# A bias subtraction in two parts, a low part ahead of statistics, a weight split behind a wait, and an activation copy moved by one place

## The reference

```
x = layernorm0( attn0(x, ctx) @ Wo + bo + x ) * gamma + beta     # 32 heads of 16, 8 key/value heads, mask
for i in (1, 2):                                                  # 16 heads of 128
    h = layernorm(x) * scale_i + offset_i
    q, k, v = h @ wq + bq, ctx @ wk + bk, ctx @ wv + bv
    k, v = concat(k, bias_k), concat(v, bias_v)                   # one extra key and value
    x = x + softmax(q @ k.T / sqrt(128)) @ v @ wo + bo
x = x + gelu(layernorm(x) @ w_fc1 + b_fc1) @ w_fc2 + b_fc2        # 512 -> 2048 -> 512
```

## Time and profile before

| | |
|---|---|
| time, median of 3 runs | 2440.11 us (2439.7 to 2440.71) |
| profiled execution, whole | 2439.39 us |
| its span, first to last instruction | 2437.6 us |
| TensorE busy | 2363.2 us, 97% of the span |
| TensorE idle | 74.4 us |
| VectorE, ScalarE, GpSimd busy | 50%, 36%, 33% |
| mean granted TensorE clock | 0.991 of full speed |
| moved by DMA | 120.08 MB, mean 49 GB/s |

### The profile page before, as it was taken

How to read it: one execution, slowest core, us unless ns; L and a number is a source line. 1 busy time by engine, 2 the same in 40 slices (tenths; PEclk the granted TensorE clock), 3 DMA queues, 4 the chain that set the end, 5 groups by cost and what they waited for, 6 DMA issues and landing times.

```text
span 2437.6 us, 38747 instructions
## 1 busy us (share of the span) xinstructions
PE 2363.2 (97%) x14768; PEld 2033.4 (83%) x14768; DVE 1220.8 (50%) x2037; ACT 870.0 (36%) x2511; POOL 812.3 (33%) x597
## 2 busy tenths in 40 slices
PE   7989999999999999999988899999999999999999
PEld 5768888888888888878866788888888888888887
DVE  6995333434533333465679843333354333334654
ACT  7964222222422222342379542222233222224321
POOL 6963232233422323130059542233243222322100
PEclk9999999999999999999999999999999999999999
DMA  5002111012111101211320021111111111110110
GB/s 206 10 10 83 35 41 53 34 43 74 35 35 34 43 34 42 75 44 60 112 86 9 10 83 44 42 53 50 37 57 35 35 43 34 43 52 14 61 44 35
DMA packets 37765, 120.08 MB, mean 49 GB/s; under 512 B 3616, under 2 KB 3872, under 8 KB 37664
## 3 DMA queue, kind: packets, MB, share of 16 engines
q1 hardware_dynamic: 37664, 118.69, 14.2%
HBM read 114.48 MB, written 4.19 MB: 49 GB/s over the span
## 4 chain that ended last, share of the span: by engine, by line
PE 85%; POOL 7%; DVE 3%; ACT 3%; issue 1%; DMA 0%; SPq 0%; POOLq 0%; DVEq 0%; ACTq 0%
PE PS L578 72%; PE PS L806 5%; PE PS L822 5%; PE PS L814 2%; POOL XN L429 1%; POOL W L453 1%; POOL P0D L429 1%; POOL X L463 1%; POOL HF L429 1%; POOL XN L422 1%; ACT AT L1153 1%; ACT PS L1153 1%; POOL W L386 1%; PE PS L797 1%; DVE XN L1440 1%
## 5 line engine op out<-in xcount | busy, mean ns | idle before, releaser
L578 PE MATMUL PS<-AT,W 128*128 128x512 f32 x2496 | 602.8, 392 | 1.6 <-DVE AT L1450 1.5
L578 PEld LDWEIGHTS PS<-AT,W 128*128 128x128 f32 x2496 | 468.4, 189 | 103.4 <-DVE AT L1450 4.2
L492 POOL TENSOR_TENSOR PR<-PR,RC 128x512 f32<-128x512 f32 x128 | 133.3, 1041 | 948.1 <-DVE RC L1537 948.1
L1329 DVE TENSOR_TENSOR X<-PS,X 128x512 f32<-128x512 f32 x416 | 286.1, 689 | 297.9 <-PE PS L578 288.7
L578 PE MATMUL PS<-CT,W 128*128 128x512 f32 x1632 | 407.9, 399 | 10.8 <-DVE CT L1324 10.4
L578 PE MATMUL PS<-W,CX 128*128 128x512 f32 x1632 | 397.2, 397 | 6.6 <-DVE Q L1354 4.7
L578 PE MATMUL PS<-W,CT 128*128 128x256 f32 x3072 | 386.5, 285 | 0.0
L578 PEld LDWEIGHTS PS<-W,CT 128*128 128x128 f32 x3072 | 373.3, 191 | 1.1 <-issue 0.8
L578 PEld LDWEIGHTS PS<-W,CX 128*128 128x128 f32 x1632 | 299.9, 188 | 73.7 <-issue 6.9
L578 PEld LDWEIGHTS PS<-CT,W 128*128 128x128 f32 x1632 | 298.9, 189 | 69.3 <-issue 11.1
L1180 ACT ACTIVATE CX<-PS,VEC 128x512 fp32r<-128x512 f32 x128 | 88.1, 688 | 661.9 <-PE PS L822 661.9
(11 more groups left out here) (110 smaller groups left out, 2470.2 us busy)
## 6 DMA issues: line engine op xcount, KB each, us to landing
RAW<-in_wq SPq DMA_DIRECT2D x44, 512.0 KB, 4.5
RAW<-in_wo SPq DMA_DIRECT2D x44, 512.0 KB, 3.2
RAW<-in_wk SPq DMA_DIRECT2D x40, 512.0 KB, 3.2
RAW<-in_wv SPq DMA_DIRECT2D x40, 512.0 KB, 3.6
raw_c<-in_cT SPq DMA_DIRECT2D x8, 512.0 KB, 7.4
raw_x<-in_xT SPq DMA_DIRECT2D x8, 512.0 KB, 5.6
BVR<-in_bv_rows SPq DMA_DIRECT2D x8, 512.0 KB, 3.7
X<-in_x SPq DMA_DIRECT2D x4, 1024.0 KB, 11.2
```

Of the source, the lines that this page charges most:

```text
L492: nc.gpsimd.tensor_tensor(PR[:, :, 0:P], PR[:, :, 0:P], RC[:, 0, 0:BT].unsqueeze(2).to_broadcast([P, BT, P]), ALU.mult).then_inc(norm_done, 1)
L578: ins = nc.tensor.matmul(out, lhs(c, a), rhs(c, b), start=(k == 0), stop=(k == total - 1))
L1329: V_.tensor_tensor(X[:, tile, :], PS[:, bank, :], X[:, tile, :], ALU.add).then_inc(done, 1)
```

## The change

It has four parts:

1. In stage 0's second last step GpSimd subtracts only the first 256 columns of `BVR` (`first_rows`), which the first values need. The other 768 are subtracted in one instruction after the steps, when VectorE has finished `own` for block 0; a new semaphore `low_rows` tells VectorE, which waits for it before the layer's second unit.
2. VectorE's `cxlo0` of the last unit stands ahead of `own_stats` and `variances`.
3. GpSimd's split of the first layer's first output slab waits, besides for the last output rows, for `XN` of block 0.
4. At the MLP border ScalarE copies `PT` after chunk 0 of the normalized block, and not after chunks 0 and 1.

```diff
@@ GpSimd, stage 0 @@
+                def first_rows():
+
+                    pool.wait_ge(ld_rows[0], hf * LAYERS * 32 + 32)
+                    nc.gpsimd.tensor_tensor(BVR[:, 0:256], BVR[:, 0:256], ROWV[:, 0:256], ALU.subtract).then_inc(vb_done, 1)
...
                     if s == STEPS0 - 2:
-                        sub_rows(0, 0)
+                        first_rows()
...
+                pool.wait_ge(own_done, hf * TB + 1)
+                nc.gpsimd.tensor_tensor(BVR[:, 256:1024], BVR[:, 256:1024], ROWV[:, 256:1024], ALU.subtract).then_inc(low_rows, 1)
@@ GpSimd, even() @@
                         if first and ly == 0:
                             pool.wait_ge(o0_ps, (hf + 1) * ROWS0)
+                            pool.wait_ge(xn_done, norm_index(hf, 0) * TB + 1)
                             psplit(3, lq + g)
@@ ScalarE, last_unit_to_mlp() @@
-                        norm_high(LAYERS, 0, BANKS_LAST, range(2))
+                        norm_high(LAYERS, 0, BANKS_LAST, range(1))
                         turned(n, 1)
-                        norm_high(LAYERS, 0, BANKS_LAST, range(2, 3))
+                        norm_high(LAYERS, 0, BANKS_LAST, range(1, 3))
                         cx_high(n, g, 1)
                         norm_high(LAYERS, 0, BANKS_LAST, range(3, C))
@@ VectorE, after stage 0 @@
                 own(0, 1)
                 first_values()
+                cxlo0(UNITS0 - 1)
                 own_stats(0)
                 variances(hf * 8 + 1, 1e-5)
-                cxlo0(UNITS0 - 1)
                 roots(hf * 8 + 1)
@@ VectorE, the layers @@
                     if ly == 0:
                         first_unit()
+                        dve.wait_ge(low_rows, hf + 1)
```

More of the change, by code:

```diff
@@ L183, in build @@
         xn_done, tr_ps, f_done, at_hi, at_lo = (sem(n) for n in ("xn_done", "tr_ps", "f_done", "at_hi", "at_lo"))
-        bo_tile, bo_added, vb_done = sem("bo_tile"), sem("bo_added"), sem("vb_done")
+        bo_tile, bo_added, vb_done, low_rows = sem("bo_tile"), sem("bo_added"), sem("vb_done"), sem("low_rows")
         q_ps, q_ev, k_ps, k_ev, v_ps, v_ev = (sem(n) for n in ("q_ps", "q_ev", "k_ps", "k_ev", "v_ps", "v_ev"))
```

## The result

The change takes 2432.08 us (median of 8 runs, 2431.43 to 2435.75) against 2439.9 us before (8 runs): a ratio of 0.9970, with a 95% interval of 0.9959 to 0.9981, 7.8 us faster. In a later comparison it was 2432.3 against 2440.39, a ratio of 0.9967 (0.9955 to 0.9979). The forecast was 2434.9, in a range of 2431.6 to 2437.7. The direction and the range held; the gain is 2.6 us larger than the 5.2 of the forecast, and its interval, 4.6 to 10.0 us, holds both values.

The account below looks back on a forecast made before the run. TensorE, 85% of the chain of waits, bounds the kernel; only its idle and low-clock time can be won. Ramps 2.5 + 1.9 and borders 0.8 make 5.2 us, giving 2434.9 us, range 2431.6 to 2437.7.

Parts of the forecast that it names:

- Part 3, the split behind XN: Both ramps: the four normalizations take 1.92 instead of 4.33 us, so XN is turned 2.5 and 3.6 us earlier.
- The 0 booked for it: Split now over block 1's statistics and small NT: no cost taken, at most 0.4 us for each half, never a gain.
- Part 2, the low part first: Both ramps: the 3.18 us wait before L711 goes; the chain to XN gains 0.1 us, in the second half 1.16.
- the 0.2 us to 168.17: First ramp: gain from the first values' old end, 168.17, to the high part CX's end, 167.98.
- Part 1, the subtraction in two: Ramp: NS is free some 1.8 us earlier, but CX's high part comes later, so worth only 0.2 us.
- The clock: TensorE at the ramps: one low stretch in each, as before, now behind XN in the second half; 1.7 us a stretch.
- the deduction of 1.7 us: Second ramp: the low stretch now falls behind XN, where all counts, so 3.6 - 1.7 = 1.9 us gained.
- Part 4: MLP borders: the wait for PT is 1.0 instead of 2.33 us; 0.8 and 0.6 us gained, 0.8 of 1.4 booked.
- the 0.6 us taken off for it: MLP borders: 0.8 of 1.4 us booked, because a late low clock stretch would cost its whole 1.7 us in the projection.
- the normalizations are slow for another reason than GpSimd: Rival, L1440 at the ramps: 2 x 2.41 us missing, 0.4 us gained, 2439.7 us; chance 0.07.
- The clock did not move into the MLP's projection: Rival, both borders: the low clock moves into the projection, 2.4 us gained, 2437.7 us; chance 0.13.
- The slower case: Rival, ramps and borders: low clock stretches multiply, slower from the fourth added one, about 2441.3 us; chance 0.03.

Follow-up runs that it names:

- the change without part 3: The change with the split's wait for XN taken out again; ratio 0.9994 (0.9985 to 1.0003) against the kernel before, 2437.15 against 2439.11 us.
- part 3 alone: The kernel before with only the slab's split made to wait for XN; ratio 0.9971 (0.9959 to 0.9982), 2432.56 against 2439.07 us.
- part 2 alone: The kernel before with only CX's low part moved ahead of the statistics; ratio 1.0000 (0.9991 to 1.0009), 2439.51 against 2439.07 us.
- parts 1 and 3 alone: The change without the early low part and without the moved PT copy; ratio 0.9945 (0.9931 to 0.9958) against the kernel before, 2426.65 against 2440.39 us.

## Why the prediction was right, step by step

- **Part 3, the split behind XN.** Right in size: XN was turned 2.63 and 3.69 us earlier, forecast 2.5 and 3.6, and the four L1449 took 1.90 us. The split's subtraction held up the small NT of block 1 (0.81 us from 178.66, which ends with GpSimd's at 179.44) and nothing else; the statistics beside it took their usual 2.46 us, and the queries did not wait. The 0 booked for it held. Parts 2 and 3 depend on each other in a way the prediction did not see: with part 2, the split would have stood over the factors and not over the normalizations, and the size came out the same.
- **Part 2, the low part first.** The step that says this edit gives 0.1 us on the chain that ends last, and 1.16 in the second half, is right for the edit made to the kernel before (0.05 and 1.03 us to XN), and wrong for what it does in the change: with part 1 in place it costs 1.4 us to XN in each half, and leaves the one long wait behind which the clock falls. Taking it out makes the change 6 to 7 us faster: 2.8 us to XN, the rest the low stretches behind it (the way to the queries is 1.4 and 4.2 us shorter than in the first profile of the change). The prediction had all the numbers: the first values end at 166.4 and CX's high part comes at 167.98. It booked the 0.2 us to 168.17 and did not ask what VectorE could do in the 1.6 us between the two.
- **Part 1, the subtraction in two.** "This alone gives TensorE nothing", 0.2 us, is wrong. Alone it gives 5.4 us, of which the profile shows 1.64 and 2.67 to XN. The prediction looked at the wait before L711, which does have ScalarE's high part as its floor, and left out that the statistics begin where the first values end. In the sum this error and the one on part 2 cancel, because the prediction worked out the two together: the change without part 3 turned XN 0.05 and 1.13 us earlier than before, where it had 0.1 and 1.16. That the sum came right in spite of two wrong attributions is luck as far as each part is meant.
- **The clock.** One low stretch in each ramp was assumed, with 1.7 us more in the second half. The two profiles of the change had none and two, and one and two. The price of a stretch, and that it stands behind the wait before XN, were right; how many there are in an execution could not be known from one profile. The count was wrong in both, and the deduction of 1.7 us is borne out by neither as it stands (the second ramps lost 2.9 us to it, the first 0 and 1.5).
- **Part 4.** 0.74 and 0.58 us at the marks, where 0.8 and 0.6 were worked out, but by luck. The step that fails is "The high part CX [...] can start there, 0.7 to 0.8 us earlier". It took ScalarE's 0.68 and 0.49 us of waiting before CX for the price of PT's place. They were the low clock of the weighing, which the prediction called free ("Before, the low clock lay where TensorE waited for low parts anyway"). At full clock and in the old order there is no such wait, and the border takes 14.88 us against 14.77: the order gives 0.1 us, and the rest is a low stretch that part 4's kernels did not have in sixteen borders. The clock worked the other way from what was feared, and the 0.6 us taken off for it were not needed.
- **The size.** 5.2 us forecast, 7.8 measured, with an interval that holds both. By the marks, 0.5 of the difference is part 4's deduction and 0.2 the ramps. What is left may be noise or clock: in stage 0 the profile of before has seven low stretches (one of double length counted as two) and those of the change four and seven. It is not settled which.
- **The rivals.** That the normalizations are slow for another reason than GpSimd fell with part 3 alone. The clock did not move into the MLP's projection. The slower case did not come (its 2441.3 does not follow from its own terms, 2440.1 + 1.0, or + 1.6 with the booked 0.6 gone; nothing hangs on it). The small NS took 0.65 us, where near 0.5 was expected.

## What to carry to other kernels

When an engine is waited for and stands idle itself, look at what is behind it in its queue: moving the awaited instruction to the front took away one wait of 3.2 us and lengthened the next from 2.4 to 5.5, and in the change four statistics that could have filled 1.44 us of idle time stood behind it. Judge each part of a change with the others in place and without them, since two errors of attribution can cancel in a sum. And before a wait is booked as a gain, look at the clock of the instructions around it, and at the same place in another execution: ScalarE's 0.68 us at the MLP border were TensorE's low clock, and an edit that seemed to win them wins 0.1. A wait costs more than it lasts if TensorE's clock falls behind it, as it did behind most of those of 2.4 us and more in these ramps and behind none of those of 1.75 and less.

## What the runs showed of the hardware that was not expected

- GpSimd's hold on VectorE does not ask how small VectorE's instruction is. RS, a 128x4 instruction with two inputs in SBUF, took 2.23 us beside GpSimd's subtraction (part 2 alone) and 0.16 us elsewhere (at 171.21 in the change); CX's low part, with one input in PSUM, and the statistics, with one input, kept their time: in the change 0.75 us at 149.74, with GpSimd's L429 from 148.81 to 150.71, and 2.46 us at 175.64, with its L379 from 177.05 on. The Trainium skill (SBUF — State Buffer, "Who interferes with whom") says that a VectorE instruction with two SBUF inputs contends with GpSimd's reads, and one with at most one SBUF input, outside the two-port modes, does not; the rows agree. NT in the run of part 2 alone waited 0.5 us beside GpSimd's plain copy (173.00 to 174.05), so a copy (line 386) holds it too.
- A clock stretch can double: 0.50 from about 1380 to 1387 us behind a single wait of 2.95 us, 2.9 us of loss, in the second ramp of both profiles of the change. The two waits of before, 3.03 and 1.97 us, had one stretch.
- An engine that is made earlier may find another one not moved. At the MLP border VectorE's weight copy (line 377) took 1.69 us after and 0.90 before, since GpSimd's subtraction (1040.19 to 1042.59 us, the copy from 1041.44) now covered more of it; before, it had run from 1046.12 to 1048.52 and the copy from 1048.17. This is not part 4's order either: in the kernel with parts 1 and 3 alone the copy took 1.60 us. TensorE had no wait behind it.
